# A graph attention layer on one core: float copies of the one-hots kept in the one-hots' own order, and TensorE's weights read across them

## The reference

```python
# x: (6250, 96) f32; rows = src, cols = dst: 200000 edges; 4 heads of 24
q = (x[rows] @ qW).reshape(e, 4, 24)
k = (x[cols] @ kW).reshape(e, 4, 24)
v = (x[cols] @ vW).reshape(e, 4, 24)
exp_s = exp(clip(einsum('ehd,ehd->eh', q, k), -10, 10))
w = exp_s / (segment_sum(exp_s, rows)[rows] + 1e-8)
res = segment_sum(w[:, :, None] * v, rows).reshape(6250, 96)
out = layernorm(x + (x + res))
```

## Time and profile before

| | us |
|---|---|
| median of 3 runs | 2211.66 (2199.44 to 2214.01) |
| the profiled execution, its own time | 2204.64 |
| its span | 2202.8 |
| PE / PEld busy | 1696.1 / 1587.8 |
| DVE busy | 1520.8 |
| ACT busy | 1162.7 |
| POOL busy | 1035.2 |
| DMA, mean | 214 GB/s |

### The profile page before, as it was taken

The page is one execution under the profiler, slowest core; times in us unless marked ns, Lnnn a source line. Parts: engine busy times, 40 slices in busy tenths (PEclk is TensorE's granted clock), DMA queues, the critical chain, the costliest instruction groups (busy, mean ns, idle before and its releaser), DMA issues.

```text
span 2202.8 us, 65205 instructions
## 1 busy us (share of the span) xinstructions
PE 1696.1 (77%) x21980; PEld 1587.8 (72%) x21981; DVE 1520.8 (69%) x3655; ACT 1162.7 (53%) x2254; POOL 1035.2 (47%) x963
## 2 busy tenths in 40 slices
PE   2936776777777677777767749999999999999991
PEld 2715666766666566666666649999999999999991
DVE  3696555555656555565655438888888888888887
ACT  2423333333333333333333338888888888888881
POOL 4223555555555655555555534444444444444440
PEclk9657787787878878787877779999999999999996
DMA  9315666666666656576666667777777777777751
GB/s 331 92 65 182 215 221 236 206 243 214 239 228 224 239 201 244 214 245 221 222 232 241 221 223 234 220 227 219 222 224 222 220 227 220 223 221 223 220 185 44
DMA packets 202553, 470.82 MB, mean 214 GB/s; under 512 B 41920, under 2 KB 74944, under 8 KB 196058
## 3 DMA queue, kind: packets, MB, share of 16 engines
q1 hardware_dynamic: 149100, 291.36, 43.0%
q0 software_dynamic: 47040, 164.33, 19.2%
q10 hardware_dynamic: 6384, 14.75, 1.8%
HBM read 281.07 MB, written 202.00 MB: 219 GB/s over the span
## 4 chain that ended last, share of the span: by engine, by line
PE 56%; another core or an unknown queue 15%; DVE 13%; issue 6%; ACT 5%; ACTq 2%; SPq 1%; DVEq 1%; DMA 0%; POOL 0%; POOLq 0%
PE meta L1127 11%; PE sum_bank L1127 10%; PE two_b L1046 7%; PE two_a L1046 7%; PE two_a L1145 5%; PE two_b L1145 5%; DVE work L1387 4%; ACT work L834 4%; PE one_c L1135 2%; PE one_d L1135 2%; PE one_d L1089 2%; ACTq L795 1%; DVE work L1381 1%; PE one_c L1046 1%
## 5 line engine op out<-in xcount | busy, mean ns | idle before, releaser
L586 POOL DMA_INDIRECT sorted_rows<-work x588 | 619.8, 1054 | 515.6 <-ACT work L837 248.2
L643 POOL TENSOR_TENSOR work<-work 128x576 f32<-128x576 f32 x312 | 362.9, 1163 | 501.7 <-ACT work L876 501.7
L885 ACT ACTIVATE work<-work 128x768 f32<-128x768 bf16 x312 | 402.1, 1289 | 0.0
L834 ACT ACTIVATE work<-two_a 128x768 f32<-128x768 f32 x196 | 159.2, 812 | 430.8 <-remote 251.2
L1046 PE MATMUL two_a<-work 128*128 128x192 bf16 x2352 | 275.6, 275 | 94.4 <-DVE work L1356 46.9
L1366 DVE TENSOR_TENSOR work<-sum_bank,run_col 128x3 uint32<-128x3 f32 x196 | 31.6, 161 | 409.4 <-remote 218.3
L1046 PEld LDWEIGHTS two_a<-work 128*128 128x128 f16 x2352 | 219.6, 109 | 111.9 <-issue 102.3
L1046 PE MATMUL two_b<-work 128*128 128x192 bf16 x2352 | 272.7, 275 | 32.8 <-ACT work L834 30.6
L1127 PE MATMUL meta<-work 128*128 128x100 f32 x1872 | 243.5, 280 | 43.9 <-issue 38.0
L1127 PEld LDWEIGHTS meta<-work 128*128 128x128 f32 x1872 | 222.0, 192 | 61.8 <-issue 61.6
L1046 PEld LDWEIGHTS two_b<-work 128*128 128x128 f16 x2352 | 230.0, 110 | 50.4 <-ACT work L834 40.7
(11 more groups left out here) (231 smaller groups left out, 2971.9 us busy)
## 6 DMA issues: line engine op xcount, KB each, us to landing
work<-sorted_rows SPq DMA_DIRECT2D x624, 294.0 KB, 3.0
work<-sorted_local SPq DMA_DIRECT2D x49, 1152.0 KB
work<-kv_table SPq DMA_DIRECT2D x196, 144.0 KB
sorted_rows<-pad_rows ACTq DMA_DIRECT2D x7, 2058.0 KB, 20.7
sorted_rows<-work POOLq DMA_INDIRECT x588
kv_table<-work SPq DMA_DIRECT2D x12, 576.0 KB, 3.4
work<-in_x SPq DMA_DIRECT2D x12, 192.0 KB, 3.6
out<-acc SPq DMA_DIRECT2D x4, 576.0 KB
```

The costliest lines, as they stand in the source:

```text
L586: pool.indirect_dma_start(out=rows_dram, out_offset=bass.IndirectOffsetOnAxis(ap=place_now[:, u, b:b + 1], axis=0), in_=payload[:, u, b * ...
L643: pool.tensor_tensor(now[:, :, 0:D].rearrange("p c (h f) -> p c h f", h=HEADS), blk[:, k, :, :, D:2 * D].rearrange("p m c (h f) -> p (m c) ...
L834: act.activation(payload[:, u, 4 * part:4 * part + 4, 0:2 * D].rearrange("p (b k) w -> p b k w", b=2), kv_ps[part], ACT.Copy).then_inc(pay ...
L885: act.activation(hot_f[:, k % HOTF], hot[:, k % HOTS].rearrange("p n c -> p c n"), ACT.Copy).then_inc(hotf_made[k % PSEM], 1)
```

## The change

The f32 copy keeps the order of `hot`: `hot_f` is now [128 nodes, 6 chunks]. The copy at L885 reads and writes 768 elements side by side. The weights of a chunk at L1127 are 128 f32 elements that lie 6 elements, 24 bytes, apart. Nothing else differs: the number of instructions, their order on each engine, their waits, and the sizes of all buffers are those of before.

```diff
-        hot_f, at = share(at, [HOTF, CH, P], F32)
+        hot_f, at = share(at, [HOTF, P, CH], F32)
...
-                        act.activation(hot_f[:, k % HOTF], hot[:, k % HOTS].rearrange("p n c -> p c n"), ACT.Copy
+                        act.activation(hot_f[:, k % HOTF], hot[:, k % HOTS], ACT.Copy
                                        ).then_inc(hotf_made[k % PSEM], 1)
...
                             for c in range(BLK):
-                                mm = pe.matmul(sums[k % 2][:, m, :], hot_f[:, k % HOTF, m * BLK + c, :],
+                                mm = pe.matmul(sums[k % 2][:, m, :], hot_f[:, k % HOTF, :, m * BLK + c],
                                                msg[:, k % MSGS, m * BLK + c, :], start=(c == 0), stop=(c == BLK - 1))
```

## The result

| | before | changed |
|---|---|---|
| median us | 2212.84 (2199.44 to 2215.55, 4 runs) | 2609.24 (2607.11 to 2610.8, 4 runs) |
| profiled execution, span | 2204.64, 2202.8 | 2608.34, 2606.4 |

The changed kernel is slower: ratio 1.1795, 95% interval 1.1746 to 1.1844, 396 us between the medians.

What follows compares the result with a forecast made beforehand. PE's chain was taken to bound the second phase, weight loads pacing its sums. Load 412, wait -34, clock +31, copy 0 made +409 on 2204.64, 2614, so 2620 us for the median; range 2280 to 2760.

Steps and rivals of the forecast that it cites:

- PE's chain bounds, the weight load paces the sums: Second phase: PE alone sets the pace, 2.50 us a pair; weight loads at L1127, every 0.112 us, pace the sums.
- The copy, 0 on the path: L885 on ACT: about 0.80 us instead of 1.289, 153 us less copying, none of it on the path.
- The load, +0.110 us each: L1127 on PE: 3744 strided weight loads at 0.222 us instead of 0.112, +412 us on the chain.
- The row that I took as nearest: L960, weights and columns 16 bytes apart: 1.81 ns a column, giving 0.232 us for a load at L1127.
- 0.218 from 0.107 doubled to two visits: L1127: of a load's 0.112 us, the 0.107 that scales with the clock doubled, giving 0.218 us.
- L1135 and L960 fit together: Weight reads: moving on by 16 bytes or so costs; 12-byte steps share it partly, 16-byte and 24-byte steps never.
- The wait for DVE, -34: PE before the sums: slower sums end the wait for DVE's addition, 0.22 us per two pairs, -34 us.
- The clock, +31: Transposes and q on PE: about 1.0 us more a pair at the low clock, for a tenth of pairs, +31 us.
- The sum: Whole kernel: 412 - 34 + 31 + 0 = +409 us, so a median of 2620 us, 18% slower.
- Reading hides in the load: Rival at L1127: strided reading costs nothing, loads stay at 0.112 us, no change; chance 0.14.
- A little of it: Rival at L1127: 27 to 54 ns more a load, 2279 to 2380 us, up to 2450; chance 0.12.
- The heavy case: Rival at L1127: 0.265 us a load, 2751 us, or 2700 to 2870 with more low clock; chance 0.09.

Runs made afterwards that it cites:

- e6: The changed kernel, but odd pairs move only 50 of the 100 columns at L1127, weights still across: 2339.3 us.
- e7: The kernel before, weights side by side, but odd pairs move only 50 of the 100 columns at L1127: 1902.9 us.
- e1: The kernel before with the fast copy alone, PE still loading 128 weights side by side: 1907.2 us, ratio 1.001.
- e3: The changed kernel with weights of even pairs 8 bytes apart and of odd pairs 12 bytes apart: 2022.6 us.
- e4: The changed kernel with weights of even pairs 16 bytes apart and of odd pairs 20 bytes apart: 2322.6 us.
- e10: The changed kernel without float copy: bf16 one-hots as weights 12 bytes apart, messages in two bf16 parts, HOTS 8: 2391.2 us, ratio 1.2555 to the kernel before.
- e13: The changed kernel with no edit, run again on a chip with a shorter first phase: 2304.5 us, ratio 1.209 to the kernel before.
- e2: The kernel before with only PE's weights read 24 bytes apart, ACT's copy and layout as before: 2301.7 us, ratio 1.2082.

## Why the prediction was right, step by step

- **PE's chain bounds, the weight load paces the sums.** Right; e6 and e7 show the second half.
- **The copy, 0 on the path.** Right (e1). Its size was 0.836 us and not 0.80: 312 x 0.453 = 141 us of copying saved instead of 153.
- **The load, +0.110 us each.** Right, and the term that carries everything: groups of 12 take 2.75 or 2.76 us, so a load 0.221 to 0.222, and 3744 x (0.222 - 0.112) = 412 us, just the term predicted. On the chain a group is 2.71 instead of 1.38, so 312 x 1.33 = 415. The row that I took as nearest, L960, was the right one. Its 16-byte step gave 1.81 ns a moving column, and the table has the same 1.81 ns at the same step for weights; no run tells whether L960's columns or its weights set its pace, nor whether it was the reading. The other number beside it, 0.218 from 0.107 doubled to two visits, was my estimate and no run shows it. What the runs show is that 12 loads side by side take 1.42 us at a granted 1.00 and 2.68 at 0.50 (the kernel before, at 1704.30 and 1323.51), and across 2.75 at both (e6, at 1504.44 and 1549.90). That 12 bytes share the cost partly, 16 and 24 never, is what e3, e4 and the changed kernel show for f32.
- **"L1135 and L960 fit together."** This step does not hold, and here the forecast had luck. L1135's bf16 weights, 12 bytes apart, lie in 96 stretches, which at 1.8 ns would take 0.17 us; they were loaded every 0.056 us in the trace before already, and e10 has 0.045. A row of f16 (L960) gave the price of f32 loads, and two rows of bf16 do not follow it. Why, stays open.
- **The wait for DVE, -34.** In the main right, but smaller: the 0.05 of issue and the 0.17 are gone in 117 places, 117 x 0.22 = 26 us. In the other 39 the 1.55 stood behind the group's issue and not behind DVE, and there it is still 2.90 against 2.72.
- **The clock, +31.** Mis-sized. I had put a tenth of the pairs at the low level, which was an estimate: no run shows what sets the granted clock. 15 of 312 have a spell, of 0.67 us in q and mostly 0.30 in the transposes, 13 us in all. The kernel before had one such spell, of about 2 us, at the start of the phase. So the term was +11. e6 shows that it was not idle: with a granted 0.90 it cost 33 us more. The 0.214 us of the term is a load side by side at a granted 0.50, (2.85 - 0.50) / 11, with 0.50 us for one duration; that sums with weights across cost the same at the low level is what e6 shows with its 2.75.
- **The sum.** 415 - 26 + 11 = 400. The kernel before also waited once, 3.6 us at the start of its second phase, which the changed one did not: 396. Between the first and last of the sums the second phase grew from 2154.9 - 1308.2 = 846.7 to 2557.3 - 1314.7 = 1242.6, so by 396. Against the 409 predicted, the load was 3 too low, the wait gave back 8 less, the clock was 20 too high, and the 4 of that single wait were not in it: the errors partly cancel, and part of the closeness is luck.
- **The rivals.** "Reading hides in the load" (the load stays at 0.112 us, the time at 2212) is out: the load took 0.221. It would have been nearly right at a step of 8 bytes, 0.118 in e3. "A little of it" took L1135's extra 27 ns as the price; a bf16 load is no measure of a f32 one at the same step (0.045 us in e10, 0.174 in e3). The heavy case took L960's weights as the pace of that loop; its 0.265 us was reached at no step up to 32 bytes.

## What to carry over

Before a layout is turned to make an idle engine's access side by side, find which engine's access becomes strided and whether that engine sets the pace: here 141 us of copying came off one that nobody waited for, and 412 went onto the one on the chain. For strided f32 weights count the 16-byte stretches they lie in, times 1.8 ns, against what the load takes side by side, 0.112 us here at a granted clock of 1.00; bf16 weights 12 bytes apart did not pay that (e10), so measure the type that you use. Where two engines are nearly even, look for the order of an engine's step that takes its wait off the loop; that gave the 2% that the copy did not.

## What was not expected of the hardware

- The same program's first phase was about 300 us shorter on the three chips of the experiments than in the first runs. The stretch from 400 to 900 us, of the kernel before in the first runs and then of the changed kernel in e13, lies in that phase, where both run the same instructions:

```profile
400.00:900.00 500.00, 362.81 (x4682) 331.43 (x4680) 284.40 (x727) 183.81 (x417) 280.65 (x265) 0.80 0.64 226
```

```profile
400.00:900.00 500.00, 427.22 (x6458) 413.43 (x6456) 388.71 (x1009) 252.60 (x577) 387.22 (x365) 0.94 0.89 312
```

  In the same time 1.38 times the bytes are moved, 312 against 226 GB/s. No run tells why.
- A bf16 load of 128 weights 12 bytes apart goes every 0.045 us, a f32 load at the same step every 0.174.
- With fewer moving columns a kernel was slower (e6), at a lower granted clock, 0.90 instead of 0.98. This is one execution; e2 and e13, with the same slow loads and all 100 columns, were granted 0.98.
